# Attention in tiles of 4 heads x 32 queries, turned by VectorE instead of TensorE, with new orders for every engine

## What is computed

```python
xn = ln(x, g_norm)
q = (xn @ Wq).reshape(b, n, HEADS, DIM_HEAD).transpose(0, 2, 1, 3)
kv = xn @ Wkv
k, v = (kv[..., :DIM_HEAD], kv[..., DIM_HEAD:])
...                                   # a null key and value go ahead of k and v: n + 1 = 129 keys
q = l2norm(q) * q_scale
k = l2norm(k) * k_scale
sim = jnp.einsum('bhid,bjd->bhij', q, k) * SCALE
sim = sim + attn_bias                 # a bias by head and by i - j, made by a small MLP of 255 positions
causal = jnp.triu(jnp.ones((n, n + 1), dtype=bool), k=2)
sim = jnp.where(causal, neg, sim)     # query i sees the null key and keys 0 to i
...
attn = jax.nn.softmax(sim, axis=-1)
out = jnp.einsum('bhij,bjd->bhid', attn, v)
out = out.transpose(0, 2, 1, 3).reshape(b, n, HEADS * DIM_HEAD)
return ln(out @ Wout, g_out)
```

## Time and profile before

| | us |
|---|---|
| runs | 812.65, 814.14, 814.35 |
| median | 814.14 |
| span of the profiled execution | 811.5 |
| PE busy in it | 777.8 (96%) |
| DVE busy | 581.3 (72%) |
| ACT busy | 602.6 (74%) |
| POOL busy | 460.3 (57%) |

### The profile page before, as it was taken

How to read it: one execution, slowest core, us unless ns; L and a number is a source line. 1 busy time by engine, 2 the same in 40 slices (tenths; PEclk the granted TensorE clock), 3 DMA queues, 4 the chain that set the end, 5 groups by cost and what they waited for, 6 DMA issues and landing times.

```text
span 811.5 us, 16623 instructions
## 1 busy us (share of the span) xinstructions
PE 777.8 (96%) x5322; PEld 593.4 (73%) x5322; DVE 581.3 (72%) x1575; ACT 602.6 (74%) x1647; POOL 460.3 (57%) x388
## 2 busy tenths in 40 slices
PE   6979988999999999999999999999999999999997
PEld 5756566777776777677786778768776777767797
DVE  5678887968768686877768687786769785666532
ACT  2325787599748977599767987599775899699974
POOL 3027976946377564946469464756559564855200
PEclk9989999999999999999999999999999999999999
DMA  7032102000030001100030000300030000000000
GB/s 257 13 106 89 53 2 70 14 1 2 1 95 1 2 1 46 51 1 2 1 96 1 2 1 11 86 0 2 1 95 1 2 2 2 1 14 1 14 2 14
DMA packets 28917, 23.41 MB, mean 29 GB/s; under 512 B 2192, under 2 KB 26400, under 8 KB 28448
## 3 DMA queue, kind: packets, MB, share of 16 engines
q1 hardware_dynamic: 28528, 22.33, 9.1%
q10 hardware_dynamic: 304, 0.01, 0.0%
HBM read 20.10 MB, written 2.24 MB: 28 GB/s over the span
## 4 chain that ended last, share of the span: by engine, by line
PE 68%; DVE 13%; POOL 7%; issue 5%; ACT 1%; DVEq 0%; POOLq 0%; ACTq 0%
PE ps_M L1243 33%; PE ps_S L1369 6%; PE ps_T L1384 6%; PE ps_z L1397 5%; PE ps_T L1377 5%; DVE sb_sm L1131 5%; PE ps_M L1429 3%; PE ps_M L1296 3%; POOL sb_sm L660 2%; PE ps_S L1351 2%; POOL sb_biasm L653 2%; DVE sb_hT L1043 2%; POOL sb_rq L643 1%; PE ps_M L1326 1%; DVE sb_bs L1033 1%
## 5 line engine op out<-in xcount | busy, mean ns | idle before, releaser
L660 POOL TENSOR_TENSOR sb_sm<-sb_sm,sb_rden 128x512 f32<-128x512 f32 x128 | 146.2, 1145 | 155.6 <-DVE sb_rden L1144 155.6
L759 ACT ACTIVATE sb_sm<-sb_sm,sb_nmx 128x129 f32<-128x129 f32 x512 | 200.1, 397 | 28.4 <-DVE sb_nmx L1139 28.0
L653 POOL TENSOR_TENSOR sb_biasm<-sb_bias,sb_maskn 128x512 f32<-128x512 f32 x128 | 168.8, 1326 | 57.3 <-DVE sb_sm L1131 36.7
L1131 DVE SCALAR_TENSOR_TENSOR sb_sm<-ps_S,sb_rq,sb_biasm 128x129 f32<-128x129 f32 x512 | 141.0, 345 | 24.0 <-PE ps_S L1369 20.1
L643 POOL TENSOR_TENSOR sb_rq<-sb_qss,sb_mhalf 128x16 f32<-128x16 f32 x32 | 93.2, 2938 | 21.9 <-DVE sb_qss L1116 21.9
L759 ACT ACTIVATION_READ_ACCUMULATOR sb_sm<-sb_sm,sb_nmx 128x1 f32 x512 | 99.1, 193 | 0.0
L1369 PEld LDWEIGHTS ps_S<-sb_k,sb_qs 64*128 64x128 f32 x1024 | 65.2, 187 | 40.7 <-issue 38.4
L773 ACT ACTIVATE sb_pT<-ps_T 128x512 f32<-128x512 f32 x128 | 74.8, 593 | 26.8 <-PE ps_T L1377 26.8
L1139 DVE TENSOR_REDUCE sb_nmx<-sb_sm 128x4 f32<-128x516 f32 x128 | 86.2, 682 | 1.4
L1369 PE MATMUL ps_S<-sb_k,sb_qs 64*128 64x129 f32 x1024 | 83.0, 291 | 3.8 <-DVE sb_sm L1131 2.2
L1377 PE MATMUL ps_T<-sb_ident,sb_sm 128*128 128x128 f32 x512 | 77.1, 276 | 3.7 <-POOL sb_sm L660 3.5
(11 more groups left out here) (260 smaller groups left out, 1770.2 us busy)
## 6 DMA issues: line engine op xcount, KB each, us to landing
sb_hA<-routes SPq DMA_DIRECT2D x48, 128.0 KB, 3.6
sb_xg<-in_xT SPq DMA_DIRECT2D x8, 256.0 KB, 4.1
sb_xs<-in_x SPq DMA_DIRECT2D x8, 256.0 KB, 4.6
sb_qs<-in_xT SPq DMA_DIRECT2D x1, 2048.0 KB, 10.2
sb_hA<-in_h SPq DMA_DIRECT2D x2, 1024.0 KB, 5.2
out_y<-sb_res SPq DMA_DIRECT2D x7, 256.0 KB, 3.9
sb_sm<-toeplitz SPq DMA_DIRECT2D x1, 1024.0 KB, 5.8
sb_rows<-in_rows SPq DMA_DIRECT2D x1, 648.0 KB, 6.1
```

What stands on the lines that cost most here:

```text
L653: pool.tensor_tensor(biasm[:, heads, 1:NK], bias0[:, heads], maskn[:, j // 4].unsqueeze(1).broadcast_to([128, 4, S]), ALU.add)\
L660: pool.tensor_tensor(sm[:, heads, 1:NK], sm[:, heads, 1:NK], rden[:, heads].unsqueeze(2).broadcast_to([128, 4, S]), ALU.mult)\
L759: ins = act.activation(sm[:, h], sm[:, h], ACT.Exp, bias=nmx[:, h:h + 1], accum_out=den[:, h:h + 1])
L1131: ins = dve.scalar_tensor_tensor(sm[:, h], bank(g, "sim", n, odd)[:, m * NK:(m + 1) * NK], rq[:, k * HEADS + h:k * HEADS + h + 1], biasm[: ...
```

## The change

- **Tiles.** A unit is now 4 heads x 32 queries (blocks of queries in the order 0, 3, 1, 2), on 128 partitions, and its keys go only to the block's end: 33, 65, 97 or 129 columns. Scores come in two bursts of 16 records per batch element instead of three. The score pass, maxima, exp, the sums and POOL's two passes work on the narrower tiles; `sm` becomes a ring of 3 buffers of two units each.
- **Turn.** PE's transposes and ACT's copies of them (PT) go. DVE's 32x32 transpose (`tp`, one or two instructions per unit, 5 per batch element, 160 in all) turns the normed tiles into `pT`, also a ring of 3: 128, 512, 256 and 256 + 128 columns per batch element.
- **P times V.** 14 matmuls per batch element instead of 4, of 256 or 128 columns, in two halves of the array's rows. The stationary operand is `vblk`, where the values stand block-diagonally. It is cleared once by POOL and filled for each group by a new SP step `vb`: 16 DMAs, after the shifted values (DVE's `vs`) and after the last PV of the former group. PV waits for them, and `vs` waits for those of the former group.
- **q sums.** 8 matmuls of 512 columns instead of 32 of 128; their PE turn and its scaling become one DVE transpose.
- **Bias.** The toeplitz load is 16 DMAs instead of one, there are 3 flips instead of 4, and 4 small loads bring the null bias. `Wq` and `Wout` are permuted on the host.
- **PSUM.** Three M banks and four S banks; PV uses S.
- **Orders.** All texts of ORDER are new. On ACT, `pb.4` stood right after `exp.4` and now stands behind `qkv.0`.

The core of the diff:

```diff
     "sp start": """
-        maskn.0 rw.0 hw.1 wb.0
+        rw.0 hw.1 maskn.0 vb.0 wb.0
     """,
     "sp steady": """
-        rw.0 maskn.0 wb.0 l4.0
+        rw.0 maskn.0 l4.0 vb.0 wb.0
     """,
...
     "pe steady": """
-        sim.0 exp.0-1 sim.1 exp.2-3 sim.2 exp.4 down.0 PT.0 zT.0 sim.3 PT.1 qkv.0 l1.0-1 PT.2-3 l1.2-3 sim.4
...
+        sim.0-1 exp.0-4 down.0 sim.2 zT.0 sim.3 qkv.0 l1.0 sim.4 l1.1 PV.0 l1.2-3 scores.0 PV.1 sim.5 l2.0-2 z.0
+        mix.0 l2.3 z.1 sim.6 PV.2-3 sim.7 l3.0-2 xnT.0 l3.3 q.0 kv.0 z.2 l4.0 q.1-3 PV.4-5 q.4 z.3 qs.0-3 PV.6-7
+        q.5-7 z.4-5 qs.4-7 kT.0 z.6-7
...
-            sp.dma_start(turned_bias, bass.AP(tensor=toeplitz.tensor, offset=0,
-                                        ap=[[1, 128], [2 * S, HEADS], [1, S]])).then_inc(s_toepl, 16)
+            for c in range(4):
+                for i in range(4):
+                    src = bass.AP(tensor=toeplitz.tensor, offset=4 * c * 2 * S + S - QW * (i + 1),
+                                  ap=[[1, QW], [2 * S, 4], [1, QW * (i + 1)]])
+                    sp.dma_start(relative(turned_bias, i)[c * QW:(c + 1) * QW], src).then_inc(s_toepl, 16)
...
+            def spread_values(g, k):
+                sp.wait_ge(v_shifted.sem, v_shifted.at(g, 1))
+                if g == 0:
+                    sp.wait_ge(v_cleared, 1)
+                sp.wait_ge(pv_psum.sem, pv_psum.at(g, 0))
+                for i in range(4):
+                    for c in range(4):
+                        sp.dma_start(vblk[c * QW:(c + 1) * QW, :, i, c % 2 * DH:(c % 2 + 1) * DH], vs[i * QW:(i + 1) * QW])\
+                            .then_inc(v_spread.sem, 16)
...
             def values_shift(g, k):
                 dve.wait_ge(kv_copied.sem, kv_copied.at(g, 1))
-                dve.wait_ge(pv_psum.sem, pv_psum.at(g, 0))
+                dve.wait_ge(v_spread.sem, v_spread.at(g, 0))
...
+            def p_turn(g, j):
+                n, (i, wide, _) = j // 2, unit(j % 4)
...
+                dve.wait_ge(p_normed.sem, p_normed.at(g, j + 1))
+                dve.wait_ge(pv_psum.sem, pv_psum.at(g, n + 1 - RING))
+                p = scored(g, j)[:, :, 1:wide].rearrange("p t (c k) -> p t c k", k=QW)
+                turned = pT[:, (g * GB * NB + n) % RING].rearrange("p (c t k) -> p t c k", t=4, k=QW)
+                if i == 2:
+                    dve.transpose(turned[:, :, 1:4:2], p[:, :, 0:2])
+                    ins = dve.transpose(turned[:, :, 4:5], p[:, :, 2:3])
...
+                for c in range(hi + 1):
+                    both = c <= lo
+                    for r in range(2):
+                        half = slice(64 * r, 64 * r + 64)
+                        dst = ps[r][:].rearrange("p (i q) -> p i q", i=4)
+                        dst = dst[:, lo:hi + 1:hi - lo] if both else dst[:, hi]
+                        src = pT[half, ring, first:first + (256 if both else 128)]
+                        ins = pe.matmul(dst, vblk[half, k, c], src, start=(c == 0), stop=(c == hi), skip_group_check=True)
+                    first += 256 if both else 128
```

More of the change, by code:

```diff
@@ L45 @@
 SPAN = 32
-BURSTS = ((0, 3), (3, 6), (6, 8))
-NB = len(BURSTS)
-LAST_BURST = (0, 1, 1, 2)
+QW = 32
+BLOCKS = (0, 3, 1, 2)
+PAIRS = (BLOCKS[0:2], BLOCKS[2:4])
+NB = len(PAIRS)
+WIDE = [QW * (i + 1) + 1 for i in range(4)]
+HALF = 4 * (WIDE[0] + WIDE[3])
+TURNED = 5 * 128
+RING = 3
 LN_EPS = 1e-5
@@ L234, in uses @@
         return "S" if k == 0 else ""
+    if step == "PV":
+        return "SS" if k % 2 == 0 else ""
     rings = "MM" if step == "exp" and (k == NX - 1 or g > 1) else USES.get(step, "")
@@ L613, in null_bias @@
             def null_bias(g, k):
-                pool.wait_ge(load["rows"], 16)
-                pool.tensor_copy(biasm[:, :, 0], nbias)
+                pool.wait_ge(nb_loaded, 4 * 16)
+                for u in range(4):
+                    pool.tensor_copy(masked_bias(u)[:, :, 0], nb[:])
             def rsqrt(which, ln, n):
@@ L889, in null_key @@
                 if k == 0:
+                    dve.wait_ge(load["rows"], 16)
                     link(dve.tensor_tensor(nks, nkey_r, nkey_r, ALU.mult), null_sum)
@@ new lines, in score @@
+                    for j in (2 * n, 2 * n + 1):
+                        i, wide, _ = unit(j % 4)
+                        for m in range(2):
+                            t, col = 2 * m + odd, k * HEADS + 4 * i + 2 * m + odd
+                            ins = dve.scalar_tensor_tensor(scored(g, j)[:, t], bank(g, "sim", n, odd)[:, first:first + wide],
+                                                           rq[:, col:col + 1], masked_bias(j % 4)[:, t], ALU.mult, ALU.add)
+                            first += wide
@@ L1218, in warm @@
                 for n in range(2):
-                    pe.matmul(banks["T", 0][:, 0:128], ident[:], ident[:], start=True, stop=True)
+                    pe.matmul(banks["S", 2][:, 0:128], ident[:], ident[:], start=True, stop=True)
             def pos_bias(g, k):
@@ L1227, in pos_bias @@
                     pe.wait_ge(load["pw1"], 16)
-                    pe.matmul(banks["S", 1][:, 0:128], ph[2], pw1[:], start=True, stop=True).then_inc(pp, 1)
+                    pe.matmul(banks["S", 1][:, 0:128], ph[2], pw1, start=True, stop=True).then_inc(pp, 1)
                 else:
@@ new lines, in pv @@
+            def pv(g, n):
+                k, ring = n // NB, (g * GB * NB + n) % RING
+                lo, hi = PAIRS[n % NB]
+                if n % NB == 0:
+                    ps = [free(g, "PV", n, r, (v_spread, 16 * 16), (p_turned, 2 * n + 2)) for r in range(2)]
+                else:
+                    pe.wait_ge(p_turned.sem, p_turned.at(g, 2 * n + 2))
+                    ps = [bank(g, "PV", n - 1, r) for r in range(2)]
+                first = 0
+                for c in range(hi + 1):
[7 more added lines that the diff above has]
+                    first += 256 if both else 128
```

370 lines of the change are left out of this document (186 added, 184 removed).

## The result

The changed kernel takes 863.35 us (median of 4 runs, 862.4 to 864.75), the kernel before 813.57 in the same comparison: ratio 1.061, 95% interval 1.060 to 1.063. It is slower, by 50 us. The prediction was 828 with a range from 800 to 852. The side and the place of the loss were right; the size was not, and the time lies 11 us above the range. The profiled execution has a span of 861.3 us and a mean granted clock of 0.934 (0.994 before).

The account below looks back on a forecast made before the run. PE's queue was taken to set the pace in six of eight iterations. Span 811.5 - 68 (PE) + 9 (DVE) + 59 (SP queue) + 8 (first boundary) + 6 (fill) = 825.5, so median 828 us; range 800 to 852.

Parts of the forecast that it names:

- PE per group: PE's work per group: transposes gone, fewer score bursts, dearer PV bursts; -8.5 us a group, -68 in all.
- DVE's tightness: DVE at 84% of an 84.7 us period makes PE idle: +5 us first iteration, +4 the others, +9 in all.
- The sum of the two, -59: PE's saving of -68 us and the +9 charged for DVE being close to the bound.
- rival 4: PE's PV row pairs do not overlap: 1.08 us more a burst, +69, 897 us; chance 0.06.
- rival 2: PE's scores are paid by columns, not by a weight load floor: -21 us, 807; chance 0.13.
- DVE, right in price: DVE's 32x32 transposes cost one pass over the columns, 7.7 us a group; DVE goes from 69.1 to 70.8.
- SP, the step that was mis-sized: Sixteen block loads and weights delay x on SP's queue: 9.8 us at each of six boundaries, +59.
- the prediction's chain: At a boundary, x issued at E + 12.8, landed at E + 16.9, experts from E + 18.3 us; PE idle 8.8.
- PE ready after: PE's own work at a boundary, q projections to two score bursts, lasts until E + 9.5 us.
- DVE's backlog: At each boundary DVE comes out of the x wait with the score pass still to do: 1 us more.
- The fill: Late toeplitz loads delay PE's flips and the turn of normed x, +6 us; block loads before the first experts, +8.
- The forecast case: The predicted 828 us, with 806 to 850 as its own range from issue price, transposes and fill; chance 0.50.

Follow-up runs that it names:

- experiment 2: Changed kernel with both the routing weights and the x load issued ahead of the sixteen block loads on SP: 770.42 us, ratio 0.944 to the kernel before.
- experiment 9: experiment 2 and experiment 3 together, x ahead of the weights in iteration 0, null-bias loads behind the large first loads: 753.26 us, ratio 0.927 to the kernel before.
- experiment 6: Kernel of experiment 2 with every score matmul only 33 columns wide, output not the reference's: 769.25 us.
- experiment 5: Kernel before the change with sixteen useless small DMAs of differing form ahead of the routing-weight loads on SP, at six places: 873.16 us, ratio 1.074.
- experiment 8: Kernel of experiment 2 with only the fill's bias step put earlier on PE and ACT: 767.01 us.
- experiment 3: Changed kernel with the fill's orders on PE, ACT, DVE and POOL as in the kernel before, SP's order kept: 857.0 us.

## Why the prediction was wrong, and what in it was right

**PE per group, nearly right.** I had -8.5 a group and a middle period of 84.7 without the queue. Experiment 2 has 85.4, and PE's busy time fell from 92.0 to 84.7, by 7.3 and not 8.5. DVE's tightness, put at +9, was too much by about as much. The sum of the two, -59, is then met by experiment 9 (814 to 753 us, with neither the queue nor the fill in the way), but by two errors that cancel: that is luck. The score burst was put at 1.09 and measured 1.07 to 1.09; the PV burst at 1.39 less what neighbours save, measured 2.39 for two in a row (249.43 to 251.82 in the changed kernel). Row pairs overlap (rival 4 is out), narrower scores give nothing (rival 2 is out, experiment 6).

**DVE, right in price, too high in effect.** The changed kernel has five forms of the transpose; two of them:

```profile
L1198 DVE STREAM_TRANSPOSE sb_pT<-sb_sm 128x512 f32<-128x512 f32 x32 | 22.1, 690 | 1.5 <-POOL sb_sm L706 1.5
L1194 DVE STREAM_TRANSPOSE sb_pT<-sb_sm 128x128 f32<-128x128 f32 x32 | 8.6, 268 | 0.0
```

690 ns for 512 columns is what the earlier trace rows gave for another operation of that length; all five sum to 67.7 us, 8.5 a group of records that overlap a little, where I had 8.4 less the overlap. DVE's total is 67.4 a period; I had 70.8. The score pass and the maxima fell by 3.4 each, as forecast. What I had not in the sum is that operations of DVE which the change doesn't touch got shorter beside a POOL that works 43 instead of 57 us a period: the last residual went from 1445 to 760 ns, the first from 1142 to 776, one low part (`hBl`) from 999 to 741, another (`hAl`) the other way, from 719 to 862. No run tests the cause. That the price is one pass over the columns agrees with what the Trainium skill states in "Vector Engine (DVE) Microarchitecture Reference", section 3.8. The +9 for DVE's tightness was too much: the middle period shows 0.8 of idle on PE (1.2 before), and the first iteration is 64.2 us in experiment 9 against 69.9 before.

**SP, the step that was mis-sized.** The order of events was as forecast, step for step, also that the last iteration is spared. Each boundary was put at 9.8 us; experiment 2 against the changed kernel gives 14 to 15 (period 99 to 101 against 85.4), and the prediction's chain can be checked term by term at the boundary shown above (E is 251.97 here):

| term | predicted | measured |
|---|---|---|
| sixteen issues | 7.5 | 10.3 |
| eight weight loads | 5.3 | 5.2 |
| x: landing, ACT, DVE, steps | 5.5 | 6.2 |
| last PV to experts | 18.3 | 21.8 |
| PE ready after | 9.5 | 9.3 |
| idle time of PE | 8.8 | 12.5 |
| DVE's backlog | 1.0 | none seen |
| lost clock behind the gap | not in the sum | 2.7 |

Two terms make the miss: the price of an issue, 0.47 us in the sum and 0.64 to 0.68 measured, and the lost clock, which the sum put at nothing. The issue price was read from the first loads of the earlier trace rows (they are fifteen, 0.49 us apart, not fourteen at 0.47). All of them have their source in DRAM; the new ones read SBUF, and experiment 5 shows 0.67 for those. The row that I used was of another kind, and I named the 0.65 of the weights only as an upper bound. And the clock: after each idle time of about 12.5 us PE's next matmuls came at half the pace. The earlier trace rows show a clock of 1.00 in two windows where PE's rests are short, so they gave no warning of the price, but the fill of the kernel before has slow stretches that I didn't look at. Over the six boundaries the issues take 10.3 to 10.9 us, 18 more than forecast, and the experts 1.4 to 2.8 us more than without a gap, 12 in sum: together 31 of the 35 us between forecast and result. The rest is smaller: the fill 5 more, the steps of x 4 more, DVE's backlog of 6 not there.

The sentence of the Trainium skill that I weighed there ("DMA: Bandwidth & Descriptors", Issuing engines are not separate DMA queues: time to initiate is usually small against the DMA) does not carry to this case. The page of the changed kernel has, for a block load, 1.9 us from issue to landing, and the issue itself takes 0.64 of it (10.31 / 16 in the rows of SP above):

```profile
sb_vblk<-sb_vs SPq DMA_DIRECT2D x128, 32.0 KB, 1.9
```

A third of one, and sixteen in a row are 5 times the landing.

**The fill, right by place, with a term missing.** I had +14 for the first experts of iteration 0, measured +19.4 (94.2 against 74.8). The experiments divide it. Taking x from behind the block loads brings them to 85.8 (experiment 2): 8.4, where I had 8, though not at the times that I had; the loads began at 79.4 instead of 75.6, and PE was ready at 86.3 instead of 80.5. The early bias step brings them to 81.6 (experiment 8): 4.2, where I had 6; the wait at the flips was 7.09 us, I had about 9. The last 6.8 were not in the sum, and they come before all of it: the new order puts the logits of all groups (L1267) first, which need the x of all groups.

```profile
18.39 3.58 PE L1267 MATMUL ps_z<-sb_wt,sb_qs 128*128 128x8 f32 x16 [5.80 <-DMA sb_qs<-in_xT]
...
31.64 0.78 PE L1299 MATMUL ps_M<-sb_xh,sb_wguh 128*128 128x512 f32 x1
32.21 0.63 PE L1299 MATMUL ps_M<-sb_xl,sb_wguh 128*128 128x512 f32 x1
```

5.8 us of waiting, and behind it again matmuls at the slow pace, until 34 us. The first expert matmul comes at 31.6 instead of 21.3. The old orders bring it to 24.3 (experiment 3). Another part is the four small loads of the null bias, which the new kernel issues ahead of larger ones:

```profile
3.25 1.82 SPq L527 DMA_DIRECT2D sb_nb<-in_rows  x4
```

Experiment 9 has them behind, and the matmul comes at 21.5. Reading the order from the first row on, and not only around the moved bias step, would have shown it. The old order hid that load behind the warming matmuls and the bias.

**The chances.** The forecast case was the one that happened, at a time that its own range (806 to 850) didn't reach. That bound used 0.65 an issue (+20), about what was measured, but had no term for the clock and none for the logits.
